# A state-space scan and an expert layer in one kernel: one block for both stages, and another order of work ahead of the first scan

## The reference

```
xz = x @ in_proj_w.T + b ;  x_in, z = split(xz)          # 512 channels each
x_conv = silu(causal_conv4(x_in) + conv_b)
dt_low, B, C = split(x_conv @ x_proj_w.T)                 # 64, 16, 16
dt = softplus(dt_low @ dt_proj_w.T + dt_proj_b)
h[t] = exp(dt*A) * h[t-1] + (exp(dt*A)-1)/A * B * x_conv  # 512 channels x 16 states
y = (sum_s h*C + D*x_conv) * silu(z)
x1 = layernorm(x + y @ out_proj_w.T + b)
out = layernorm(x1 + shared_mlp(x1) + sum over the 2 best of 16 experts of w_e * mlp_e(x1))
```

## Time and profile before

| | us |
|---|---|
| median of 3 runs | 2208.38 |
| profiled execution, its own time | 2207.55 |
| its span in the trace | 2205.7 |
| ahead of the first scan | 57.40 |
| the 16 units of scans | 57.40 to 1846.2 |
| from the last work of DVE in the scan stage to the first work of PE in the slot stage | 1846.2 to 1854.5 |
| ahead of the first slot tile | 1854.5 to 1880.3 |
| slot tiles | 1880.3 to 2115.8 |
| shared expert, last norm | 2115.8 to 2205.7 |

### The profile page before, as it was taken

The page is one execution under the profiler, slowest core; times in us unless marked ns, Lnnn a source line. Parts: engine busy times, 40 slices in busy tenths (PEclk is TensorE's granted clock), DMA queues, the critical chain, the costliest instruction groups (busy, mean ns, idle before and its releaser), DMA issues. The chain is left out here.

```text
span 2205.7 us, 68576 instructions
## 1 busy us (share of the span) xinstructions
PE 2053.2 (93%) x26550; PEld 1252.6 (57%) x26550; DVE 1826.8 (83%) x3055; ACT 1782.1 (81%) x3561; POOL 1775.2 (80%) x1699
## 2 busy tenths in 40 slices
PE   6899999999999999999999999999999897999996
PEld 2455555555555555555555555555555554889964
DVE  2898999989998989888989898889898995555556
ACT  4888888888888888898989897979898873677747
POOL 2787898979897989898989898889898985576654
PEclk9999999999999999999999999999999998999999
DMA  2232333333333233333232333233333355497668
GB/s 90 69 101 78 110 97 110 92 107 97 111 93 115 88 115 93 110 90 118 88 118 90 112 90 117 83 111 95 108 99 99 92 161 179 120 282 217 208 213 286
DMA packets 152304, 267.46 MB, mean 121 GB/s; under 512 B 26408, under 2 KB 65324, under 8 KB 151470
## 3 DMA queue, kind: packets, MB, share of 16 engines
q1 hardware_dynamic: 137198, 220.93, 33.2%
q0 software_dynamic: 14784, 42.16, 5.4%
HBM read 205.62 MB, written 57.39 MB: 119 GB/s over the span
## 5 line engine op out<-in xcount | busy, mean ns | idle before, releaser
L617 POOL TENSOR_TENSOR hc<-h,c_rep 128x512 f32<-128x512 f32 x1024 | 1284.9, 1276 | 208.7 <-DVE h L1175 167.1
L1175 DVE TENSOR_TENSOR_SCAN h<-g_ps,carry,h 128x512 f32<-128x512 f32 x1024 | 1273.9, 1272 | 71.7 <-ACT h L691 52.4
L691 ACT ACTIVATE h<-dt,a_mat 128x512 f32<-128x512 f32 x1024 | 694.9, 714 | 107.5 <-POOL hc L617 44.0
L969 PEld LDWEIGHTS g_ps<-b_steps,x_conv_rows 64*64 64x64 f32 x16384 | 477.8, 134 | 296.4 <-issue 207.3
L969 PE MATMUL g_ps<-b_steps,x_conv_rows 64*64 64x128 f32 x16384 | 560.3, 274 | 27.2 <-DVE h L1175 21.8
L930 PE MATMUL y_ps<-hc,dg_inv 64*64 64x512 f32 x2048 | 501.3, 604 | 13.6 <-DVE y_gated L1182 5.8
L931 PE MATMUL y_ps<-hc,dg_inv 64*64 64x512 f32 x2048 | 499.9, 604 | 0.0
L930 PEld LDWEIGHTS y_ps<-hc,dg_inv 64*64 64x64 f32 x2048 | 139.4, 135 | 231.7 <-issue 156.8
L1661 POOL DMA_INDIRECT y_planes<-gathered,home x144 | 139.7, 970 | 100.5 <-DVE gathered L2094 78.9
L1867 PE MATMUL banks<-gathered,w_now 128*128 128x128 f32 x1152 | 155.2, 278 | 4.0 <-ACT w_now L1729 3.4
L1867 PEld LDWEIGHTS banks<-gathered,w_now 128*128 128x128 f32 x1152 | 141.2, 193 | 6.6 <-issue 5.9
(11 more groups left out here) (275 smaller groups left out, 2864.1 us busy)
## 6 DMA issues: line engine op xcount, KB each, us to landing
c_rep<-bc_rows SPq DMA_DIRECT2D x512, 256.0 KB
gathered<-slot_rows SPq DMA_DIRECT2D x144, 129.5 KB, 3.5
gathered<-y_planes SPq DMA_DIRECT2D x32, 512.0 KB, 8.5
w_up<-in_x_t SPq DMA_DIRECT2D x16, 512.0 KB, 4.8
x_raw<-in_x_tok SPq DMA_DIRECT2D x16, 512.0 KB, 5.0
out<-x_t SPq DMA_DIRECT2D x16, 512.0 KB, 3.2
x_t_rows<-y_gated SPq DMA_DIRECT2D x15, 512.0 KB, 4.6
x_t<-x_t_rows POOLq DMA_DIRECT2D x12, 512.0 KB, 5.3
```

The source lines that it names most:

```text
L617: nc.gpsimd.tensor_tensor(hc[:, at_all % HCS], h[:, at_all % SLOTS], c_rep[:, at % CS], ALU.mult).then_inc(hc_ready, 1)
L691: nc.scalar.activation(h[:, (ITEMS * u + m) % SLOTS], dt[:, c], ACT.Exp, scale=a_mat[:, c, s:s + 1]).then_inc(factor_ready, 1)
L969: one = nc.tensor.matmul(g_ps[some, e, r * T + k * P:r * T + (k + 1) * P], x_rows[rows, c, k, some], steps_of, start=True, stop=True)
L1175: nc.vector.tensor_tensor_scan(slot, du, slot, carry[:, batch(u), c, s:s + 1], ALU.add, ALU.mult).then_inc(scanned, 1)
```

## The change

One block holds both stages; the barrier between them is gone, and the second function appends to the same engine programs. In its place each engine waits for what it needs.

```diff
+        def mamba_left(eng):
+            eng.wait_ge(kept.gated, CH * UNITS)
+            eng.wait_ge(kept.carried, QUADS * UNITS - 1)
+            for q in range(2):
+                eng.wait_ge(kept.emptied[q], kept.in_work[q])
+        def weights_in(eng):
+            eng.wait_ge(kept.up_in, 16 * UP_LOADS)
+            eng.wait_ge(kept.down_in, 16 * LOADS)
```

Pass -1 and unit 0 get tables of their own:

```diff
+        PLACE_FIRST = [('x0', 3), ('x3', 4), ('x1', 4), ('x2', 5), ('c0', 11), ('c1', 11), ('c2', 21), ('c3', 21),
+          ('low', 27), ('T1', 30), ('bc', 34), ('d0', 34), ('d1', 34), ('X0', 38), ('X1', 41), ('T0', 43), ('e', 44),
+          ('a0', 55), ('b0', 55), ('a1', 56), ('b1', 56)]
+        PLACE_SECOND = [('d2', 1), ('d3', 1), ('T2', 2), ('c0', 3), ('c1', 3), ('z3', 8), ('Y2', 8), ('a3', 11), ('z0', 11),
+          ('T3', 12), ('b3', 13), ('a2', 15), ('b2', 16), ('z1', 18), ('Y3', 19), ('r0', 22), ('r1', 22), ('z2', 23), ('c2', 27),
+          ('c3', 27), ('low', 35), ('r2', 39), ('r3', 39), ('d0', 43), ('d1', 43), ('X2', 46), ('bc', 47), ('X0', 52), ('a0', 55),
+          ('X3', 55), ('e', 55), ('T0', 58), ('a1', 58), ('b0', 59), ('b1', 59), ('X1', 60), ('T1', 61)]
+        STEPS_FIRST = [31, 60, 69, 64, 70, 67, 83, 89]
+        SILU_FIRST, SKIP_ROWS_AT, TURN_AT, FILL_FIRST = (22, 31), 39, 7, 56
+        Z_FIRST, SQUARES_FIRST, ENDS_FIRST, BOTH_FIRST = 41, 47, 60, 18
```

```diff
+                if u < 0 and m in SILU_FIRST:
+                    half = 2 * SILU_FIRST.index(m)
+                    emptied_all(act, u, [f"c{c}" for c in (half, half + 1)])
+                    two = x_conv[nq][:, half:half + 2]
+                    nc.scalar.activation(two, two, ACT.Silu).then_inc(x_conv_ready, 1)
...
+            def take_x(t):
+                c, bank = int(t[1]), bank_of(-1, t)
+                dve.wait_ge(filled[bank], tiles_before(-1, t) + 1)
+                dve.wait_ge(halo_moved, 2)
+                nc.vector.tensor_scalar(x_in[:, c, HALO:], work[:, bank], b_in[:, c:c + 1], None, ALU.add).then_inc(emptied[bank], 1)
...
-            pe.wait_ge(early_in, 16 * len(EARLY))
+            pe.wait_ge(early_in, 16)
...
+                    if u == -1 and c == 0:
+                        pe.wait_ge(later_in, 16 * (len(LATER) + 5))
```

More of the change, by code:

```diff
@@ L361, in parts_of, with where, later @@
             return PARTS.get(t, PARTS.get(t[0], 1))
+        def where(u, t):
+            return places_in(u)[order_in(u)[t]][1]
+        def later(u, t):
+            return (LATER_FIRST if u < 0 else LATER_SECOND if u == 0 else LATER_BY).get(t, 0)
         def held(u):
-            return [t for t, _ in PLACE if (t in FIRST and u < 0) or (t in AFTER_NEXT and u < UNITS - 2) or (t in NEXT and u < UNITS - 1) or (t in OWN and u >= 0) or (t in ROUTING and u > 0)]
+            return [t for t, _ in places_in(u) if (t in FIRST and u < 0) or t in ALSO_NEXT or (t in AFTER_NEXT and u < UNITS - 2) or (t in NEXT and u < UNITS - 1) or (t in OWN and u >= 0) or (t in ROUTING and u > 0)]
         FIRST_TILE = {}
@@ L408, in x_taken @@
             if n > 0:
-                emptied_all(eng, n - 2, [f"X{c}" for c in some])
+                also = [f"Y{c}" for c in some if n == 1 and f"Y{c}" in ALSO_NEXT]
+                if also:
+                    emptied_all(eng, 0, also)
+                rest = [f"X{c}" for c in some if f"Y{c}" not in also]
+                if rest:
+                    emptied_all(eng, n - 2, rest)
             else:
@@ L420, in due, with steps_due @@
                     if (at - m) % ITEMS == 0 and 0 <= u - (at - m) // ITEMS < UNITS]
-        EARLY = ["w_in", "b_in"]
-        SMALL = ["taps", "a_log", "b_conv", "b_dt"]
+        def steps_due(m, u):
+            return [(su, j) for su, j in due(STEPS_AT, m, u) if su > 0] + [(su, j) for su, j in due(STEPS_FIRST, m, u) if su == 0]
+        SMALL = ["b_in", "taps", "a_log", "b_conv", "b_dt"]
         LATER = ["w_dt", "w_out", "b_out", "w_gate", "b_gate"]
@@ L859, in weave @@
                 for t in taken_at(u, m):
-                    if t[0] != "o":
+                    if t[0] != "o" and not (u < 0 and t in AFTER_NEXT):
                         tile(u, t)
@@ L901, in _ @@
                     if u == -1 and m == 40:
-                        act.wait_ge(turned_inv, 1)
                         act.wait_ge(a_inv_step, 5)
-                        for at in (0, HALF_ROWS):
-                            nc.scalar.activation(skip_rows[at:at + NS], y_ps[0:NS, 0], ACT.Copy, scale=-1.0).then_inc(skip_rows_ready, 1)
                         act.wait_ge(routing_made, 7)
@@ L1258, in weave @@
                         softplus(u, t)
+                    if u < 0 and t in AFTER_NEXT:
+                        take_x(t)
+                if u < 0 and m == SKIP_ROWS_AT:
+                    dve.wait_ge(turned_inv, 1)
+                    for at in (0, HALF_ROWS):
+                        nc.vector.tensor_scalar(skip_rows[at:at + NS], y_ps[0:NS, 0], -1.0, None, ALU.mult).then_inc(skip_rows_ready, 1)
                 if u >= 0 and m in SKIP_AT:
@@ L1799, in up_early @@
                 one.then_inc(up_ready, 1)
+            mamba_left(pe)
             turn_following()
@@ L1963, in write_rows @@
                 done(V.tensor_copy(row[:, first:first + tiles], row_f[:, at]))
+            mamba_left(dve)
             dve.wait_ge(made, TABLES_MADE)
```

124 lines of the change are left out of this document (79 added, 45 removed).

## The result

| | before | after |
|---|---|---|
| median of 6 runs each | 2208.89 us | 2196.73 us |
| lowest, highest | 2208.31, 2215.46 | 2190.98, 2200.48 |
| profiled execution | 2207.55 us | 2190.98 us |

The ratio of the times is 0.9937, 95% interval 0.9917 to 0.9957: 12 us faster by the medians, 14 by the ratio, with an interval of 9.5 to 18.

The account below looks back on a forecast made before the run. Bounds: one chain from PE's first product to the first scan, PE's barrier wait at the border, PE nearly always busy in slot tiles. Front -12.0, unit 0 +2.5, border -9.4: -18.9 from 2207.55, plus 0.8, gives 2189.5 us (2182 to 2199).

Parts of the forecast that it names:

- PE's start: Pass -1: needing only half of `w_in`, PE starts at 6.1 us instead of 7.47, -1.4.
- The x tiles to `low`: Pass -1: four x tiles in 8.9 us, then the convolution pairs without pause; `low` copied at 30.4 instead of 37.93, -7.5.
- From relu to the first scan: Pass -1: from relu of d1 at 35.5 to the first scan at 45.4 us, against 57.40 before.
- T0 and e: 40.2: Pass -1: after ACT's table, sigmoid, halo and square (39.2), products T0 and e are done at 40.2 us.
- Unit 0: First unit of scans: gets the x tiles, takes and `b_steps` pair dropped by pass -1, +2.5 us (bounds -2 and +6.9).
- the new places remove waits: Unit 0's lower bound: the new order removes waits, so the unit gets 2 us shorter.
- The border: Between scan and slot stages: barrier wait gone (-8.3) and a faster first projection (-1.1), together -9.4 us.
- All else PE needs at its start is old: Border: PE's start is held only by DVE's last product, everything else being ready earlier; behind the -8.3 us.
- without the stretch it is near the second: Border: without PE's idle stretch the first projection, 3.20 us, comes near the next one's 1.89, -1.1.
- slots waiting for POOL: Rival, border: POOL's second copy lands late, PE waits ahead of the first slot; 2198 us, 0.09 with no effect.
- no effect: Rival, border: the slot stage's first instructions still wait for POOL's end; 2197 us, 0.09 together with slots waiting for POOL.
- Units 1 to 14: Later scan units: not edited, but shifted clock dips move the time by ±3 us for one, ±6 for two.

Follow-up runs that it names:

- e7: Changed kernel with SP's later loads (`w_x` on) held until the first half of `w_in` has landed; 2236.47 us, ratio 0.9907.
- e10: Changed kernel with silu's table loaded early, second early up products in banks of their own, SP's later loads held; 2232.55 us, ratio 0.9894.
- e12: Kernel of e11 with DVE's takes of X0 and X1 moved behind unit 0's first and second scans; 2229.58 us, ratio 0.9921.
- e11: Kernel of e10 with pass -1's T0 and e ahead of X0 and X1, these two behind the factor tiles; 2232.72 us, ratio 0.9904.
- e2: Kernel before with one block for both stages and the new waits only, old orders and loads in pass -1 and unit 0; 2205.31 us, ratio 0.9965.
- e1: Changed kernel with the barrier between the stages put back, so pass -1 and unit 0 alone; 2202.86 us, ratio 0.9954.
- e3: Changed kernel with a one-column silu on ACT ahead of its first slot-stage wait, loading silu's table early; 2191.97 us, ratio 0.9897.
- e4: Changed kernel run again without edit, on the chip of e1 to e3; 2194.96 us, ratio 0.9914.
- e9: Changed kernel without edit, third profile, on another chip than e4; 2236.73 us, ratio 0.9919.
- e6: Changed kernel with pairs 6 and 7 of `b_steps` both at item 78 in unit 0, 16 ACT instructions in a row; 2237.50 us, ratio 0.9911.
- e8: Kernel of e3 with the exp table loaded early in pass -1 and the second early up products in the projections' banks; 2236.07 us, ratio 0.9910.

## Why the prediction held, step by step

**PE's start: wrong.** Forecast 6.1, in the three profiles of the changed kernel 7.58, 6.72 and 7.50. The half of `w_in` is half the size, but it took 6.3 us from issue in the first profile, not the 4.8 of an x load, and the whole had taken 5.7. The number of loads behind it is the old one (ten by 6.7 us), but the five small ones now come from ACT's queue beside it, so that SP's larger ones follow it at once. The step that failed is taking a duration from loads with other neighbours: with the later ones held (e7, e10 to e12) PE starts at 6.1 to 6.7.

**The x tiles to `low`: nearly right.** 9.68 us instead of 8.9 for the four tiles (PE waited for ACT's takes, 0.65 and 0.75), then 0.9 to c0, 3.67 and 3.66 for the pairs and 3.68 for `low`, as forecast. `low` was copied at 32.62 instead of 30.4, and relu of d1 ended at 37.71 instead of 35.5: both 2.2 us late, and all of it is the start's 1.5 and the tiles' 0.8.

**From relu to the first scan: 11.0 instead of 9.9.** "T0 and e: 40.2" failed, which had no term for X0 and X1 on PE. PE makes them ahead of T0, in part at the low clock (5.21 us), and DVE's takes, which I had hidden, hand the banks on; b_minus ended at 43.76. e11 shows the mechanism: with these two tiles behind, the stretch from relu to the first decay's end was 1.7 us shorter than in after and 3.0 shorter than in e10, whose X tiles met more of the low clock (6.54 us). From b_minus to the scan the sum held, 4.9 us against 5.2 forecast, with `find_ends` on POOL until 46.33 and `add_relu` of the first chunk until 47.56. These two are the last links ahead of the decay (the factors of the first chunk were ready at 45.77), and no run tries them in the other order.

**Unit 0: right in what it adds, wrong in the sum.** Seven of its eight groups of eight scans took 93.2 us together, against 91.4 before and 90.8 with the same old order in e2: +1.7 to +2.4, and 93.9 to 94.3 in the other profiles with this order (e1, e3, e4, e9), so the +2.5 for the added tiles and pair was about right. The third group went the other way. What I had only as a bound ("the new places remove waits") was worth 3.3 us, ACT's sixteen instructions in a row, shown by e6. It could have been read from the trace of before: PE's wait of 3.74 us stands there.

**The border: the barrier's 8.3 and the first projection's 1.3 came; 2.7 us were lost.** 1.3 is silu's table, whose load stood ahead of ACT's wait before and stands behind it now (e1, e2, e3). 1.7 is the second group of up products at the low clock, which e3, e8 and e10 to e12 link to the longer pause that the load makes (see the clock below). "All else PE needs at its start is old" missed that ACT's hidden load is no instruction of the program. The 1.3 of the first projection came with some luck: "without the stretch it is near the second" holds in after, e4, e8, e11 and e12, but in seven of the twelve profiles without a barrier it took 3.1 to 3.3 us all the same, with PE idle for 1.41 us ahead of it and not 9.73. The two rivals, slots waiting for POOL and no effect, are out: SP's loads lay 11 us ahead, and PE began 0.06 us after `y_gated`. The forecast's scatter beside DVE is not the row at 1859.44, during which DVE was idle, but one at 1858.17, also of 0.96 us.

**The sum.** -8.7 - 1.6 + 0.8 - 6.7 - 0.4 = -16.6, against -18.9: the front and the border gave 6.0 less, unit 0 4.1 more. That the total came near rests on luck, two errors of opposite sign. The median lay 5.7 us above the profiled execution, where before it had 1.3 (2208.89 and 2207.55): that execution of after was the fastest of its six. So the runs' medians moved by 12.2 us, two thirds of the forecast, in the first comparison, and by 18.6 in e4's. Three small slips had no part in it: the front's weak bound is -7 in one place and -8 in another, the terms to 35.5 add up to 35.4, and before, the fourth X take (57.20) came behind the first decay, so that three stood on the chain, not four.

**Units 1 to 14: the noise was as described.** Units of the same work last 111.8 and 114.5 us in the windows above, at a granted clock of 1.00 and 0.97, others 112.5. Over fourteen profiles units 1 to 15 took 1681.9 to 1687.7 us, whatever the edit; before and after, at 1681.9 and 1682.7, are the two lowest. e11, e7 and e12 have three of the four earliest starts of unit 1 (152.4 to 154.4) and the three longest sums behind them, which takes back in their profiles what the front had won; the fourth, after at 153.9, has one of the shortest. Whether the one causes the other is open.

**A version that beats both?** e3 against e4: -3.0 us; e10 and e11 against e9: -4.2 and -4.0. The marks show 1.4 us at the border for e3, and 6.5 for e11 (unit 1 begins 2.75 us earlier, the border is 3.8 shorter), of which units 1 to 15 take 3.1 back in its profile; but intervals of 3 to 5 us on each side don't separate the medians. All three beat the kernel before by 21 to 24 us; that they beat the changed one is likely and not shown.

## What to carry to other kernels

When a wait or a barrier is moved, list what the engines did in its shadow, the loads of activation tables too: they appear in no line of the kernel, and a new wait ahead of an activation can put its table load behind the wait. When a first item is brought forward, look one item further: the tile that shared its bank or its queue may hold the second (e12). Compare executions whose clock did the same ahead of the stretch in question (e3). Read the longest wait of each engine in every stretch whose order changes, also where the change is meant for something else.

## What the runs showed of the hardware

**Table loads.** Each was 1.28 us, and PE's pause became 1.28 us shorter in e3. The Trainium skill ("ScalarE: Activation LUTs", section "What ACT_TABLE_LOAD costs") gives 1.283 us for the load and 2.66 with a drain behind it; here no row shows the second part: in after the silu began 0.02 us behind the load, and the next load (1850.56) began 0.01 us behind that silu, with its own activation 0.02 us behind it. The measured 1.28 decides for this place.

**The clock.** Which group of the border ran low differs, also between three profiles of one kernel with the same pauses of PE: the second up products (after), the third (e4), the first projection and the second up products (e9, rows of 3.11 and 5.37 us). But the pauses matter. The second up products ran low in seven of the eight profiles in which PE had waited 2.86 us ahead of them (all but e4), and in none of the six in which it had waited 1.58 or less (before, e3, e8, e10 to e12). The third ran low in e4, e8 and e10 to e12. Where the first projection ran low without a barrier (seven profiles), the granted clock had fallen 3.5 to 3.9 us ahead of the end of the last `y_gated`, in the scan stage. So the late load costs 1.3 us and, most times, 1.7 more; why e4 escaped no run shows. The Trainium skill ("TensorE: Matmul & The Clock Gate", section "Part 1: The HAM clock gate") says that the gate is free-running against the program; that after, e4 and e9 differ agrees with it, while the seven of eight suggest that what the program does still counts. A forecast can put this cost at some group of the border (1.2 to 1.7 us for most, 1.1 and 2.3 for the last two of e10), with a chance and not a certainty for a chosen one.

**Chips differ in one stage.** Windows of the slot tiles for the same kernel, e4's chip and then e9's:

```profile
1867.45:2103.16 235.71, 230.12 (x1750) 212.59 (x1749) 134.45 (x548) 173.19 (x438) 152.36 (x166) 0.99 0.66 201
```

```profile
1868.29:2138.80 270.51, 240.55 (x1750) 216.02 (x1749) 133.74 (x548) 169.01 (x438) 152.92 (x166) 0.97 0.59 175
```

The work of each engine is the same within 5%, and the scan stage took the same time, but the slot tiles took 35 us longer (35 to 44 over the eight profiles on the second and the third chip), with PE idle for 30 us instead of 6. In e8 PE waited, from 1900 to 2140, 16.0 us for ACT's copies of the weights, 6.0 for ACT's copies of the rows and 7.9 for nothing that the profile shows; in e4, from 1900 to 2100, only 1.7 in all. No run tells the cause. It is about twice the change's gain, so only kernels of one chip may be compared.
